# Row numbers of an edge step: spread over the partitions by TensorE, or read from DRAM as a broadcast

## The chip, the cores and the metric

One Trainium2 chip, one core of it. The metric is the device time of one execution in microseconds. The engines are TensorE (PE, with its weight loads shown as PEld), VectorE (DVE), ScalarE (ACT), GpSimd (POOL) and SyncE (SP), which here only issues DMA transfers and waits.

## The reference

The kernel computes one layer of a graph network on 6250 nodes of 256 channels with 200000 edges. Three parts are added to a residual:

```
xn = _layernorm(x, axis=-1)
x = x + _L0_gnn_ref(xn, src, dst, ...) + _L0_mix_ref(xn[None], ...)[0]
x = x + _L0_ffn_ref(_layernorm(x, axis=-1)[None], ...)[0]
```

The graph part is attention over edges: for each edge a score from its two end nodes, an exponential, and a sum of the weighted rows of one end node into the other ("row") node:

```
e = jnp.einsum('ehd,hd->eh', Wh_i, a_src) + jnp.einsum('ehd,hd->eh', Wh_j, a_dst)
e = jax.nn.leaky_relu(e, negative_slope=ALPHA)
e = jnp.exp(e - jnp.max(e, axis=0, keepdims=True))
e_sum = jax.ops.segment_sum(e, edge_row, num_segments=N)
alpha = e / (e_sum[edge_row] + 1e-15)
h_new = jax.ops.segment_sum(Wh_j * alpha[..., None], edge_row, num_segments=N)
```

The mix part is a linear attention over all nodes with products of pairs of channels as features. The last part is a layer of 8 experts of which each node uses two.

## The kernel before

**Stages.** First the nodes are projected in 49 tiles of 128 and stored in DRAM while the edges are sorted (to about 600 us). Then comes the stage that the change touches, from about 628 us to 3670 us. The experts follow.

**The edge stage.** The sorted edges are cut into 391 groups of 512 (GE = 512, four times 128 edges). A step is a pair of a group and a tile of 128 row nodes; there are 440 steps, written as 110 laps of four (a lap's step s has slot s). Each of the five engines runs its own program over the laps, and they meet at semaphores. For step k:

- POOL gathers the 512 node rows of the group from `table` with four indirect DMAs (L805), once for each group.
- DVE makes a one-hot matrix with edges on the partitions (one_hot, L1438).
- The row numbers of the group's 512 edges, counted from the tile's first row, are wanted on every partition. `rows_b` holds them for all steps: step 4p + b lies on partition p, block b. PE spreads one partition's 512 numbers over all partitions by a product with a column of the identity (spread_rows, L1911), into `pbank[0]`.
- ACT takes them in copy_oht: `away` = |number - partition| (L1028), then 1 - away, cut at zero (L1031). That is OHT, the one-hot matrix with row nodes on the partitions. Just before, it copies the tile's table (`rowt`, L1026).
- PE multiplies OHT with the tile's table (row_scores, L1924), DVE adds the gathered scores (scores, L1455 to L1458), ACT takes exponentials (exps, L1037), DVE weighs the gathered rows (weigh, L1464), PE sums them into rows (sum_rows, L1935), and DVE adds the sums into `agg` (add, L1475).

**Order.** Within step k the engines' queues are, in this order. PE: spread_rows(k+3), sum_rows(k), row_scores(k+2), then the step's share of the mix part. ACT: copy_oht(k+3), exps(k+1), then its share. DVE: weigh(k), its share, scores(k+1), add(k-1), one_hot(k+3). Spread_rows(k) waits until ACT has read the bank for step k-1 (`rows_taken`); copy_oht waits for the product (`rows_made`). All numbers go through one bank.

**The mix part** rides on the same laps. In the first 52 laps (K laps, four times 13) SP loads tiles of `kv_dram` (load_k), DVE makes features of them (L1484 to L1487) and PE sums products (kv_part, L1944). In the next 49 laps (Q laps) SP loads from `q_dram` (load_q), DVE makes features, PE transposes them (ft_part, L1969), ACT copies the transposes (L1076), PE multiplies them (y_part, L1977 and L1980). Spread over a lap are the tail of the tile before (copies L1057, L1052 and L1065 on ACT, L1512 and L1515 on DVE) and its store (store_mix). In Q laps ft_part stands between spread_rows and sum_rows. The last nine laps, 36 steps, have edges only.

**SP's queue.** It waits in order: load_k of unit j, s may go once PE has used the unit four before it, load_q once DVE has. Parameters of the last stage are loaded between the K passes (`early`, L576).

Of the kernel before, what the change touches and what calls it, by code (L numbers as in the profile page):

```python
# [139 lines left out]
def _build(nc, t, ctx):  # L140
# [3 lines left out]
    def sem(name):  # L144
        return ctx.enter_context(nc.semaphore(name))
# [11 lines left out]
    xs_dram = [nc.dram_tensor(f"xs_dram{b}", [n, C], F32).ap() for b, n in enumerate(XROWS)]  # L157
    y_dram = [nc.dram_tensor(f"y_dram{b}", [n * P, C], F32).ap() for b, n in enumerate(BTILES)]
    sorted_dram = nc.dram_tensor("sorted_dram", [P * KEYS // GE, GE], I32).ap()

# [12 lines left out]
    rows_b = spare[:, 2 * U * P:4 * U * P].bitcast(BF16).rearrange("p (a n) -> p a n", a=4)  # L173
    ident_b = sb("ident_b", [P, P], BF16)
    away = sb("away", [P, 2, GE], BF16)
# [199 lines left out]
    oh_done = sem("oh_done")  # L375
    rows_made = sem("rows_made")
    rows_taken = sem("rows_taken")
# [128 lines left out]
    def _(sp):  # L506
# [26 lines left out]


        for i in range(2):
            sp.wait_ge(st_out[i], 48 * ((NT + 1 - i) // 2))
# [30 lines left out]

        for pair in range(PAIRS):
            for s in range(4):
                load_k(pair, 0, s)  # L570
            with sp.Fori(1, KL - 1) as j:
                for s in range(4):
                    load_k(pair, j, s)
            load_k(pair, KL - 1, 0)
            for dst, src, loaded in early[pair::PAIRS]:
                sp.dma_start(dst, src, allow_slow_non_contiguous=True).then_inc(loaded, 16)  # L576
        for s in range(4):
            load_q(0, s)
        for s in range(4):
            load_q(1, s)  # L580
        with sp.Fori(2, NT) as q:
            for s in range(4):
                load_q(q, s)
            store_mix(q - 2)
        store_mix(NT - 2)
        store_mix(NT - 1)


# [314 lines left out]
    def _(act):  # L903
# [117 lines left out]
        def copy_oht(k):  # L1021
            s = k.slot
            if k.after(4):
                act.wait_ge(s_made, k.n - 3)
            i = act.value_load(istep[0:1, bass.ds(k.n, 1)], min_val=0, max_val=AGT - 1)
            o.mark(act.activation(rowt[:, s, :], row_pl[:, bass.ds(i, 1), :, :].rearrange("p a b n -> p (a b n)"), ACT.Copy))  # L1026
            act.wait_ge(rows_made, k.n + 1)
            o.mark(act.activation(away[:, s % 2, :], pbank[0][:, :], ACT.Abs, bias=minus_p[:, 0:1]))  # L1028
            o.settle()
            act.sem_inc(rows_taken, 1)  # L1030
            act.activation(OHT[:, s, :, :].rearrange("p u n -> p (u n)"), away[:, s % 2, :], ACT.Relu, scale=-1.0, bias=ones[:, 0:1]).then_inc(oht_done, 1)  # L1031
# [185 lines left out]
    def _(dve):  # L1217
# [186 lines left out]
        dve.sem_inc(s_pint, 1)  # L1404
        o.mark(dve.tensor_copy(rows_b[:, :, :], planf[:, 1, :, :]))
        o.mark(dve.tensor_copy(ident_b[:, :], ident[:, :]))

# [419 lines left out]
    def _(pe):  # L1827
# [77 lines left out]

        def spread_rows(k):

            if k.after(1):
                pe.wait_ge(rows_taken, k.n)
            one = ident_b[:, bass.ds(k.lap, 1)].to_broadcast([P, P])  # L1910
            pe.matmul(pbank[0][:, :], one, rows_b[:, k.slot, :], start=True, stop=True).then_inc(rows_made, 1)  # L1911

        def row_scores(k):
# [90 lines left out]
        def lap(i, extra=None, middle=None):  # L2004
            for s in range(4):
                k = At(i, s, 4)
                if (k + 3).inside(STEPS):
                    spread_rows(k + 3)
                if middle is not None:
# [13 lines left out]

        for s in range(3):
            spread_rows(At(0, s, 4))
        row_scores(At(0, 0, 4))
# [169 lines left out]
```

## Time and profile before

| | |
|---|---|
| time, three runs | 4551.9, 4566.98 and 4567.17 us (median 4566.98) |
| the profiled execution | 4563.81 us |
| its span in the trace | 4561.9 us |
| mean granted clock of TensorE | 0.844 of full |
| busy: PE, DVE, ACT, POOL | 73%, 59%, 39%, 56% of the span |
| edge stage | about 628 to 3670 us |
| HBM traffic | 308.82 MB read, 84.30 MB written |

The profile is of one execution. A busy share is a mean over stages with different limits; a wait is listed with the engine and line that released it, as far as the trace can tell. "Remote" and "another core or an unknown queue" stand for a releaser that it can't name, "issue" for time in which the engine waited for nothing that the profile shows. The clock is a share of 2.4 GHz: a stretch at 0.5 is at the lower level, 1.2 GHz, and a mean between is a mixture of the two. Some matmul records can be missing from a trace.

### The profile page before, as it was taken

What the parts mean: (1) busy time and instruction counts of PE and PEld (TensorE: products, weight loads), DVE (VectorE), ACT (ScalarE), POOL (GpSimd) and SP (SyncE); (2) the same over time, 40 slices, a digit from 0 to 9 for tenths busy, and PEclk for the clock granted to TensorE, in tenths of its full rate; (3) what the DMA queues carried; (4) which work ended last, traced back from release to release, by engine and by line L of the source; (5) the groups of instructions that cost most, each with busy time, mean ns of one, the idle gap of its engine ahead of it and who ended that gap; (6) DMA issues with size and microseconds to landing.
All of it is one profiled execution on the core that took longest, in us unless ns stands there. A gap on an engine that the chain in (4) does not pass through costs nothing.

```text
span 4561.9 us, 90761 instructions
## 1 busy us (share of the span) xinstructions
PE 3309.0 (73%) x23188; PEld 2345.3 (51%) x23505; DVE 2688.7 (59%) x6015; ACT 1791.1 (39%) x4855; POOL 2546.9 (56%) x2454
## 2 busy tenths in 40 slices
PE   5888747767767777777777777777776545877895
PEld 2333324444444444456665666666564435665785
DVE  9888876657667666655555555555554463534222
ACT  3666422223323223244444444444443212543563
POOL 4566457767778867755565555555555613234223
PEclk8676668879989979889888989989897776988998
DMA  2222123333333323322222222222222232334344
GB/s 66 77 76 77 60 84 90 87 94 91 98 93 94 106 78 91 98 73 73 70 76 68 73 75 72 71 75 71 68 74 64 72 127 71 110 105 146 97 133 138
DMA packets 260611, 394.74 MB, mean 87 GB/s; under 512 B 71952, under 2 KB 195022, under 8 KB 260232
## 3 DMA queue, kind: packets, MB, share of 16 engines
q0 software_dynamic: 86704, 239.52, 18.9%
q1 hardware_dynamic: 150924, 132.95, 9.4%
q10 hardware_dynamic: 22860, 20.83, 1.6%
q8 instruction: 53, 0.87, 0.1%
q14 instruction: 70, 0.57, 0.0%
HBM read 308.82 MB, written 84.30 MB: 86 GB/s over the span
## 4 chain that ended last, share of the span: by engine, by line
PE 29%; issue 20%; DVE 13%; another core or an unknown queue 12%; DVEq 12%; ACT 7%; POOL 4%; ACTq 2%; DMA 1%; POOLq 0%; SPq 0%
PE bank L1935 6%; PE bank L1856 5%; DVEq L1445 4%; DVEq L1468 4%; PE bank L2123 3%; PE bank L2135 3%; DVEq L1444 3%; PE bank L1858 2%; PE bank L1969 2%; ACT away L1028 2%; DVE room L1438 1%; POOL room L805 1%; PE bank L1924 1%; DVE room L1464 1%
## 5 line engine op out<-in xcount | busy, mean ns | idle before, releaser
L805 POOL DMA_INDIRECT room<-table,room x1564 | 1804.0, 1153 | 1091.6 <-DVE room L1464 645.5
L1935 PE MATMUL bank<-room 128*128 128x260 f32 x3520 | 1020.7, 439 | 380.3 <-issue 208.0
L1935 PEld LDWEIGHTS bank<-room 128*128 128x128 f32 x3520 | 730.5, 218 | 512.0 <-issue 398.9
L1484 DVE TENSOR_TENSOR room<-room 128x1024 f32<-128x1024 f32 x392 | 481.2, 1228 | 533.0 <-issue 499.1
L1464 DVE TENSOR_TENSOR room<-room 128x1024 f32<-128x1024 f32 x440 | 537.0, 1220 | 389.7 <-ACT room L1037 268.4
L1028 ACT ACTIVATE away<-bank,minus_p 128x512 bf16<-128x512 f32 x440 | 301.7, 686 | 1084.7 <-remote 980.2
L1969 PE MATMUL bank<-ident,room 128*128 128x128 f32 x1764 | 262.1, 299 | 206.6 <-DVE room L1487 142.7
L1856 PE MATMUL bank<-room 128*128 128x264 f32 (+1 forms) x588 | 312.8, 673 | 65.8 <-issue 34.4
L1031 ACT ACTIVATE spare<-away,ones 128x512 bf16<-128x512 bf16 x440 | 317.6, 722 | 54.2
L1969 PEld LDWEIGHTS bank<-ident,room 128*128 128x128 f32 x1764 | 218.6, 154 | 197.1 <-issue 185.6
L1924 PE MATMUL bank<-rowt,spare 128*128 128x8 bf16 x7040 | 262.1, 167 | 73.2 <-issue 72.5
L1438 DVE TENSOR_TENSOR room<-iota_f,row_step 128x512 f32<-128x512 f32 x440 | 308.0, 700 | 0.3 <-DVE row_step L1376 0.3
L2135 PE MATMUL bank<-room 128*128 x952 | 243.4, 400 | 57.8 <-issue 22.4
L1944 PE MATMUL bank<-room 128*33 128x64 f32 (+1 forms) x1568 | 267.1, 447 | 13.2 <-DVE room L1487 6.5
L1769 DVE TENSOR_TENSOR planes<-bank,spare 128x256 f32<-128x256 f32 x119 | 50.5, 425 | 374.9 <-PE bank L2135 237.5
L1924 PEld LDWEIGHTS bank<-rowt,spare 128*128 128x128 bf16 x7040 | 214.6, 97 | 93.2 <-issue 80.8
L1076 ACT ACTIVATE room<-bank 128x512 f32<-128x512 f32 (+1 forms) x588 | 247.8, 486 | 21.1 <-remote 10.0
L1037 ACT ACTIVATE room<-room 128x16 f32<-128x16 f32 x440 | 92.2, 209 | 416.7 <-issue 188.0
L1980 PE MATMUL bank<-room,kvm 128*33 128x128 f32 x3136 | 247.1, 302 | 6.1 <-issue 5.8
L2123 PE MATMUL bank<-room 128*128 128x128 f32 x1904 | 242.0, 280 | 12.9 <-issue 12.9
L1856 PEld LDWEIGHTS bank<-room 128*128 128x128 f32 x588 | 138.8, 260 | 200.4 <-issue 144.1
L2123 PEld LDWEIGHTS bank<-room 128*128 128x128 f32 x1904 | 231.0, 197 | 12.9 <-issue 12.9
(313 smaller groups left out, 4793.0 us busy)
## 6 DMA issues: line engine op xcount, KB each, us to landing
room<-table,room POOLq DMA_INDIRECT x1564
kv_dram<-room SPq DMA_DIRECT2D x49, 324.0 KB, 2.2
room<-kv_dram SPq DMA_DIRECT2D x196, 81.0 KB
y_dram<-planes SPq DMA_DIRECT2D x119, 128.0 KB
room<-xs_dram ACTq DMA_DIRECT2D x110, 128.0 KB
q_dram<-room SPq DMA_DIRECT2D x49, 192.0 KB, 1.8
room<-q_dram SPq DMA_DIRECT2D x196, 48.0 KB
table<-room SPq DMA_DIRECT2D x49, 130.0 KB, 2.1
```

The source lines that it names most:

```text
L805: pool.indirect_dma_start(G[:, k.slot, u, :], None, table, bass.IndirectOffsetOnAxis(ap=ixbuf[:, k.slot, u:u + 1].bitcast(I32), axis=0)).t ...
L1028: o.mark(act.activation(away[:, s % 2, :], pbank[0][:, :], ACT.Abs, bias=minus_p[:, 0:1]))
L1031: act.activation(OHT[:, s, :, :].rearrange("p u n -> p (u n)"), away[:, s % 2, :], ACT.Relu, scale=-1.0, bias=ones[:, 0:1]).then_inc(oht_d ...
L1438: dve.tensor_tensor(OH[:, s, :, :], iota_f[:].unsqueeze(1).to_broadcast([P, U, P]), row_step[:, bass.ds(k.n, 1), :].rearrange("p a u -> p ...
L1464: dve.tensor_tensor(Gw[:, h, :, 0:C].rearrange("p u (h d) -> p u h d", h=GH), G[:, bass.ds(slot, 1), :, 0:C].rearrange("p a u (h d) -> p ( ...
L1484: dve.tensor_tensor(f.rearrange("p h (d i) -> p h d i", i=MD), over(x, [[XD, 2], [0, h], [1, MD]]), over(x, [[XD, 2], [1, h], [1, MD]]), A ...
L1856: ins = pe.matmul(out, xnT[:, s, c, :], w[:, c, :], start=(c == 0), stop=(c == 1 and bias is None))
L1924: ins = pe.matmul(out[:, u * w:(u + 1) * w], OHT[:, s, u, :], rowt[:, s, j * w:(j + 1) * w], start=False, stop=(j == 3), skip_group_check= ...
L1935: ins = pe.matmul(pbank[1 + h][:, 0:TW], OH[:, s, u, :], Gw[:, h, u, :], start=(u == 0), stop=(u == U - 1))
L1969: ins = pe.transpose(pbank[3 + j][:, x * P:(x + 1) * P], src, ident[:])
L2123: ins = pe.matmul(pbank[4 + n % 2][:, c * P:(c + 1) * P], w1_t[:, n % 2, kc * HID + c * P:kc * HID + (c + 1) * P], xT_t[:, n % 2, kc, :], ...
L2135: ins = pe.matmul(pbank[6 + n % 2][:, 0:C], h_t[:, n % 2, c, :], w2[:, bass.ds(e, 1), c, :].rearrange("p a n -> p (a n)"), start=(c == 0), ...
```

## The change

The row numbers no longer pass through PE. Once DVE has cast them into `rows_b`, SP writes that tile to DRAM (`rows_dram`, one line of 512 numbers for each step). For each step SP then issues one DMA that reads the step's line and writes it to all 128 partitions, into one of four slots of `rows_b`, which is used over again for this. ACT's `away` reads the slot in SBUF in place of the PSUM bank and waits for the load's semaphore (`row_in`). Load k waits until ACT has taken step k-4. The loads are placed between SP's other transfers, about one lap ahead of the step. Spread_rows, the identity in bfloat16 and the semaphore `rows_made` go.

```diff
--- before.py
+++ after.py
@@ -156,6 +156,7 @@
     x1_dram = nc.dram_tensor("x1_dram", [NP, C], F32).ap()
     xs_dram = [nc.dram_tensor(f"xs_dram{b}", [n, C], F32).ap() for b, n in enumerate(XROWS)]
     y_dram = [nc.dram_tensor(f"y_dram{b}", [n * P, C], F32).ap() for b, n in enumerate(BTILES)]
+    rows_dram = nc.dram_tensor("rows_dram", [PLAN, GE], BF16).ap()
     sorted_dram = nc.dram_tensor("sorted_dram", [P * KEYS // GE, GE], I32).ap()
 
 
@@ -171,7 +172,6 @@
     spare = sb("spare", [P, XE * C])
     OHT = spare[:, 0:2 * U * P].bitcast(BF16).rearrange("p (a u n) -> p a u n", a=4, u=U)
     rows_b = spare[:, 2 * U * P:4 * U * P].bitcast(BF16).rearrange("p (a n) -> p a n", a=4)
-    ident_b = sb("ident_b", [P, P], BF16)
     away = sb("away", [P, 2, GE], BF16)
     minus_p = sb("minus_p", [P, 1])
     rowt = sb("rowt", [P, 4, 4 * 2 * GH], BF16)
@@ -373,7 +373,8 @@
     gathered = [sem(f"gathered{i}") for i in range(4)]
     landed = sem("landed")
     oh_done = sem("oh_done")
-    rows_made = sem("rows_made")
+    s_rows = sem("s_rows")
+    row_in = [sem(f"row_in{i}") for i in range(4)]
     rows_taken = sem("rows_taken")
     oht_done = sem("oht_done")
     s_made = sem("s_made")
@@ -532,6 +533,17 @@
         sp.dma_start(sorted_dram.rearrange("(p g) e -> p (g e)", p=P), key[SORTED][:, :].bitcast(I32)).then_inc(s_sorted_out, 16)
 
 
+        def load_row(k):
+
+            if k.after(4):
+                sp.wait_ge(rows_taken, k.n - 3)
+            sp.dma_start(rows_b[:, k.slot, :], rows_dram[bass.ds(k.n, 1), :].rearrange("a n -> (a n)").partition_broadcast(P)).then_inc(row_in[k.slot], 16)
+
+        sp.wait_ge(s_rows, 1)
+        sp.dma_start(rows_dram.rearrange("(p b) e -> p b e", b=4), rows_b[:, :, :]).then_inc(s_rows, 16)
+        sp.wait_ge(s_rows, 17)
+        for s in range(4):
+            load_row(At(0, s, 4))
         for i in range(2):
             sp.wait_ge(st_out[i], 48 * ((NT + 1 - i) // 2))
         sp.wait_ge(s_plan, 1)
@@ -566,24 +578,33 @@
         early += [(w2[:, e, :, :], t["W2"][e].rearrange("(c p) n -> p c n", p=P), s_w4e) for e in range(XE)]
 
         for pair in range(PAIRS):
+            l0 = pair * KL
             for s in range(4):
                 load_k(pair, 0, s)
+                load_row(At(l0 + 1, s, 4))
             with sp.Fori(1, KL - 1) as j:
                 for s in range(4):
+                    load_row(At(j + (l0 + 1), s, 4))
                     load_k(pair, j, s)
             load_k(pair, KL - 1, 0)
+            for s in range(4):
+                load_row(At(l0 + KL, s, 4))
             for dst, src, loaded in early[pair::PAIRS]:
                 sp.dma_start(dst, src, allow_slow_non_contiguous=True).then_inc(loaded, 16)
-        for s in range(4):
-            load_q(0, s)
-        for s in range(4):
-            load_q(1, s)
+        for q in range(2):
+            for s in range(4):
+                load_q(q, s)
+                load_row(At(LAPS_K + q + 1, s, 4))
         with sp.Fori(2, NT) as q:
             for s in range(4):
+                load_row(At(q + (LAPS_K + 1), s, 4))
                 load_q(q, s)
             store_mix(q - 2)
         store_mix(NT - 2)
         store_mix(NT - 1)
+        with sp.Fori(LAPS_K + NT + 1, LAPS) as i:
+            for s in range(4):
+                load_row(At(i, s, 4))
 
 
         sp.wait_ge(s_edges_end, 1)
@@ -1024,8 +1045,8 @@
                 act.wait_ge(s_made, k.n - 3)
             i = act.value_load(istep[0:1, bass.ds(k.n, 1)], min_val=0, max_val=AGT - 1)
             o.mark(act.activation(rowt[:, s, :], row_pl[:, bass.ds(i, 1), :, :].rearrange("p a b n -> p (a b n)"), ACT.Copy))
-            act.wait_ge(rows_made, k.n + 1)
-            o.mark(act.activation(away[:, s % 2, :], pbank[0][:, :], ACT.Abs, bias=minus_p[:, 0:1]))
+            act.wait_ge(row_in[s], 16 * (k.lap + 1))
+            o.mark(act.activation(away[:, s % 2, :], rows_b[:, s, :], ACT.Abs, bias=minus_p[:, 0:1]))
             o.settle()
             act.sem_inc(rows_taken, 1)
             act.activation(OHT[:, s, :, :].rearrange("p u n -> p (u n)"), away[:, s % 2, :], ACT.Relu, scale=-1.0, bias=ones[:, 0:1]).then_inc(oht_done, 1)
@@ -1402,8 +1423,7 @@
             o.mark(dve.tensor_scalar(planf[:, 1, b, :], plan[:, b, :].bitcast(I32), pc[:, 8 + b:9 + b], None, ALU.subtract))
         o.settle()
         dve.sem_inc(s_pint, 1)
-        o.mark(dve.tensor_copy(rows_b[:, :, :], planf[:, 1, :, :]))
-        o.mark(dve.tensor_copy(ident_b[:, :], ident[:, :]))
+        dve.tensor_copy(rows_b[:, :, :], planf[:, 1, :, :]).then_inc(s_rows, 1)
 
         dve.wait_ge(qkn_done, NT)
         for i in range(2):
@@ -1903,13 +1923,6 @@
                 z = zero_b[:].unsqueeze(1).to_broadcast([P, 4, P]) if w == MAIN else zero_b[:, 0:w]
                 pe.matmul(pbank[bnk][:, 0:w], zero_b[:], z, start=True, stop=False, skip_group_check=True)
 
-        def spread_rows(k):
-
-            if k.after(1):
-                pe.wait_ge(rows_taken, k.n)
-            one = ident_b[:, bass.ds(k.lap, 1)].to_broadcast([P, P])
-            pe.matmul(pbank[0][:, :], one, rows_b[:, k.slot, :], start=True, stop=True).then_inc(rows_made, 1)
-
         def row_scores(k):
 
             s, h = k.slot, k.slot % 2
@@ -2004,8 +2017,6 @@
         def lap(i, extra=None, middle=None):
             for s in range(4):
                 k = At(i, s, 4)
-                if (k + 3).inside(STEPS):
-                    spread_rows(k + 3)
                 if middle is not None:
                     middle(s)
                 sum_rows(k)
@@ -2021,8 +2032,6 @@
                 y_part(q, s)
             return extra
 
-        for s in range(3):
-            spread_rows(At(0, s, 4))
         row_scores(At(0, 0, 4))
         row_scores(At(0, 1, 4))
         for pair in range(PAIRS):
```

## Rows read from the trace of the kernel before

**Rows 1.** The page, part 4: the chain of waits by engine
```profile
PE 29%; issue 20%; DVE 13%; another core or an unknown queue 12%; DVEq 12%; ACT 7%; POOL 4%; ACTq 2%; DMA 1%; POOLq 0%; SPq 0%
```

**Rows 2.** Busy time by stretch: us, PE, PEld, DVE, ACT, POOL, clock, DMA share, GB/s
```profile
640.00:1926.00 1286.00, 924.86 (x6850) 575.89 (x6953) 848.98 (x2055) 375.51 (x837) 960.55 (x919) 0.87 0.35 93
1940.00:3442.00 1502.00, 1151.97 (x10598) 919.97 (x10792) 849.69 (x2046) 657.57 (x1549) 839.21 (x870) 0.90 0.26 72
3457.00:3672.00 215.00, 126.91 (x872) 90.43 (x888) 96.24 (x242) 59.39 (x134) 124.75 (x138) 0.74 0.26 70
```

**Rows 3.** Waits, DVE, 640 to 1926 us: total, times, longest
```profile
DVE room L1464 <- ACT room L1037: 29.6, 18, 3.6
```

**Rows 4.** Waits, DVE, 1940 to 3442 us
```profile
DVE room L1464 <- ACT room L1037: 234.4, 78, 5.6
```

**Rows 5.** Waits, ACT, 1940 to 3442 us
```profile
ACT away L1028 <- remote: 497.1, 169, 7.9
ACT room L1052 <- remote: 65.7, 16, 5.0
ACT room L1052 <- PE bank L1996: 57.2, 27, 3.8
ACT room L1065 <- remote: 47.5, 9, 9.4
```

**Rows 6.** Line L1911: count, duration ns min/median/max
```profile
L1911 PEld LDWEIGHTS bank<-spare,ident_b x440: 95/96/152, 627.4 to 3660.3; 128*128 x133, 128*128 128x128 bf16 x14
...
L1911 PE MATMUL bank<-spare,ident_b x123: 376/390/615, 629.2 to 3657.5; 128*128 128x512 bf16 x123
```

**Rows 7.** Timeline of one Q step: start, duration, engine, [idle before <-releaser]
```profile
2486.43 0.10 PEld L1911 LDWEIGHTS bank<-spare,ident_b 128*128 x1 [0.20 <-issue]
...
2487.64 1.92 PE L1935 MATMUL bank<-room 128*128 128x260 f32 x8
...
2488.25 0.16 DVE L1458 TENSOR_TENSOR room<-room,bank 128x16 f32<-128x16 f32 x1
...
2491.33 0.69 ACT L1028 ACTIVATE away<-bank,minus_p 128x512 bf16<-128x512 f32 x1 [2.86 <-remote]
...
2492.77 0.20 ACT L1037 ACTIVATE room<-room 128x16 f32<-128x16 f32 x1
...
2493.11 1.22 DVE L1464 TENSOR_TENSOR room<-room 128x1024 f32<-128x1024 f32 x1 [3.70 <-ACT room L1037]
```

**Rows 8.** Waits, PE, 1940 to 3442 us
```profile
PE bank L1969 <- DVE room L1487: 142.0, 113, 5.5
PE bank L1977 <- ACT room L1076: 93.6, 59, 2.6
```

**Rows 9.** Line L1935 by stretch: us, PE, PEld, clock, DMA share, GB/s
```profile
640.00:1926.00 1286.00, 496.32 (x1656) 349.41 (x1656) 0.87 0.35 93
1940.00:3442.00 1502.00, 417.78 (x1560) 307.50 (x1560) 0.90 0.26 72
3457.00:3672.00 215.00, 97.91 (x277) 67.66 (x278) 0.74 0.26 70
```

**Rows 10.** Waits, DVE, 3457 to 3672 us
```profile
DVE room L1455 <- PE bank L1924: 30.2, 6, 12.5
```

**Rows 11.** The page, part 5: busy, mean ns of one, idle before
```profile
L1028 ACT ACTIVATE away<-bank,minus_p 128x512 bf16<-128x512 f32 x440 | 301.7, 686 | 1084.7 <-remote 980.2
...
L1031 ACT ACTIVATE spare<-away,ones 128x512 bf16<-128x512 bf16 x440 | 317.6, 722 | 54.2
```

**Rows 12.** DMA issues over the run: KB each, median us to landing
```profile
spare<-in_b SPq DMA_DIRECT2D x1, 1024.0 KB, 12.2
```

**Rows 13.** DMA queues, 640 to 1926 us: packets, MB, share of 16 engines
```profile
q0 software_dynamic: 35265, 97.86, 28.0%
q1 hardware_dynamic: 34384, 20.87, 6.4%
```

**Rows 14.** Waits, POOL, 640 to 1926 us
```profile
POOL room L805 <- DVE room L1464: 119.3, 24, 12.5
```

## The prediction

> **What bounds the kernel now.** I read the chain of waits over the whole run first [rows 1]: TensorE (PE) 29%, but 12% is "another core or an unknown queue", on one core. That is a wait whose releaser the trace doesn't name. The reader is to see that no engine's throughput sets the end.
>
> Then the busy time in three windows of the stage that the change touches [rows 2]: the K laps (208 steps, 1286 us, 6.2 us a step), the Q laps (196 steps, 1502 us, 7.7 us a step) and the last 36 steps (215 us). PE is busy 72%, 77% and 59% of them, VectorE (DVE) 66%, 57% and 45%. GpSimd (POOL) is busy 75% in the K laps and 56% in the Q laps. In the K laps DVE and POOL are each nearly full once their register loads and issue gaps are added; in the Q laps something else is late.
>
> Then the waits, by stage. DVE's weigh (L1464) waits for ScalarE's (ACT's) exponentials (L1037) 29.6 us in the K laps [rows 3] and 234.4 us in the Q laps, 78 times [rows 4]. Why are the exponentials late? ACT runs copy_oht(k+3) ahead of exps(k+1), and copy_oht waits for the product that spreads the row numbers: away (L1028) waits 497.1 us in the Q laps on a "remote" releaser [rows 5]. It is the product: L1911 ran 440 times and only 123 of its matmuls are recorded, so mostly the trace can't name it [rows 6]. The timeline of one Q step shows the damage [rows 7]: the weights of the product are loaded at 2486.43, the input of the exponentials (L1458) is ready at 2488.41, but away starts only at 2491.33, the exponentials at 2492.77, and weigh 3.70 us late. The product itself is 0.4 us; the hand-over from PE to ACT took 4.9 us. ACT's other waits for PE, L1052 and L1065, are late in the same manner [rows 5], so I put it down to PE's side and not to ACT's.
>
> **The change, part by part.**
>
> *The product goes* (440 times 0.39 us, the median of the recorded ones [rows 6]), and with it ACT's dependence on PE's place in its queue.
> Q laps: 234.4 us [rows 4] is the most that earlier exponentials give at weigh. ACT waits ahead of them for away (497.1) and for the tail copies (65.7 + 57.2 + 47.5 = 170.4) [rows 5]; away's share is 497/667 = 0.75, so 175 us. Not all of it survives. PE has 1502 - 1152 = 350 us of recorded idle, in which lie the unrecorded products (196 times 0.39 = 76 us); it waits 142.0 us of it for features (L1969 on L1487) and 93.6 for ACT's copies (L1977 on L1076) [rows 2, 8]. A step that is 175/196 = 0.9 us shorter uses most of what PE has free, with its issue gaps, so PE ends last in part of the steps. I take 0.7 of 175: -125 us, bounds 0 and -234.
> K laps: weigh waits 29.6 us for exponentials; I take 20. Where PE's clock is low PE can end last: sum_rows (L1935) is 300 ns here, against 240 and about 479 at the two levels (8 of them took 1.92 us in the step of [rows 7]; half the clock doubles it), so a quarter of the steps, 52, are slow, times 0.4 us is 21 us, of which I take half [rows 7, 9]. Together -30 us, bounds 0 and -50.
> Last 36 steps: L1455 waits 30.2 us for row_scores (L1924) [rows 10]. Row_scores waits for OHT, which comes after away. I take -10 us, bounds 0 and -30: that wait may also be PE's own.
>
> *PE's wait for rows_taken goes, too.* It was met early nearly always; nothing.
>
> *away now reads SBUF.* L1028 from PSUM takes 686 ns, L1031 of the same size from SBUF 722 [rows 11]: +0.036 us times 440 = 16 us on ACT, which is 29% to 44% busy in the windows [rows 2]. I take +5 us, bounds 0 and +16.
>
> *SP's loads.* 440 loads of 128 copies of 1 KB. Load k+4 is issued once away of step k is done and is needed by away of step k+4, four steps or 25 to 31 us later. The one broadcast in the trace, 1024 KB, landed in 12.2 us [rows 12]; an eighth of it is far inside the lead even if the fixed part were all of it. Behind a waiting load_row in SP's queue stand load_k or load_q and store_mix. In the loops load_k of step k was free once PE had used unit k-4; now it also waits for away of step k, which ACT does three steps before DVE wants the unit, so 18 us are left: hidden. Store_mix(NT-1) now has the last rows behind it, once; ACT needs the next row about a step later, so 0 to 5 us. At the start the row numbers go to DRAM (512 KB, half of 12.2 us by [rows 12]) and the first row comes back before the first away, while DVE makes the other tables: 0 to +8 us, I take +2. DVE's ident_b copy, under 0.3 us, goes.
>
> *The 16 DMA engines.* The SP queue's packets took 6.4% of 16 x 1286 us for 34384 packets of 607 bytes, 38 ns each; POOL's took 28.0% for 35265 of 2775 bytes, 163 ns [rows 13]. By the line between them 1 KB is 63 ns, so a row load is 128 x 63 / 16 = 0.5 us on every DMA engine, about 8 points of share on top of 35% in the K laps. The other bound is 12.2/8 = 1.5 us. The gathers share these engines. In the K laps POOL waits 119.3 us for weigh, its slack; its 919 instructions are 184 groups of one index copy and four gathers, so 0.65 us a group [rows 2, 14]. A load delays a group by 0.5 x 208/184 = 0.57 us at most by the first bound: under the slack, +5 us. I take the first because its packets are nearest in kind.
>
> Sum: -125 - 30 - 10 + 5 + 2 + 5 = -153 us. The profiled execution took 4563.8 us (span 4561.9), 3 us under the median 4567.0. **4411 us**, 3.4% faster.
>
> **The rivals.**
>
> *A. The next engine takes over.* In the Q laps DVE's features and PE's own work come next. For it: PE waits 142 us for features already [rows 8], and POOL and DVE are near full in the K laps. Against it: the K laps, with the same weigh, features and scores on DVE, take 6.2 us a step [rows 2]. Gain then about 50 us: 4515.
>
> *B. It doesn't do what it says: away stays late.* If the late start is ACT's (its sequencer) and the product only stands beside it, the wait moves to the load's semaphore. For it: 4.9 us isn't a matmul's time. Against it: L1052 and L1065, which PE releases too, wait for "remote" as well [rows 5], and in [rows 7] ACT goes from away (2491.33) to the exponentials (2492.77) in 1.44 us, which is the two passes of 0.7 us [rows 11] without a gap. 4564 plus ACT's 5: 4569.
>
> *C. The row loads hold up the gathers: slower.* Place: the K laps, where POOL is nearly full. At 1.5 us on every DMA engine a group lands 1.7 us later: 184 x (1.7 - 0.65) = +193 us, against -153 with its DMA term taken out (-158): 4599, and the more the worse. It decides from a delay of 0.65 + 158/184 = 1.5 us a group. For it: 128 reads of the same 1 KB, which the trace never shows at this rate. Against: the 16 DMA engines are 26% to 35% busy [rows 2].
> The Trainium skill, "DMA: Bandwidth & Descriptors", section "Issuing engines are not separate DMA queues", says that another issuing engine brings no DMA engines of its own; by it SP's loads and POOL's gathers compete, which is this rival, and leaves its price open.
>
> *D. PE's clock falls.* The granted clock is 0.87, 0.90 and 0.74 in the three windows, and L1935 takes 300, 268 and 353 ns [rows 2, 9]. Where PE does least (59%) it is lowest. Without the products PE is idle 5% more of a step unless the step shrinks as well. If the Q laps came halfway to the last window, PE's 1152 us grow by 0.16, 184 us, half behind DVE: +92, and the gain from an early away is half lost with it: 4564 - 90 + 92 = 4566, and as slow as 4600 with the K laps.
> The Trainium skill, "TensorE: Matmul & The Clock Gate", section "What's actually happening", says that "the default state is throttled, and activity releases the throttle". By it work taken from PE can cost clock; the sum without the rule is 4411, with it 4566.
>
> **How the numbers follow.** Chances: forecast 0.60 (its own range 4320 to 4490), A 0.15, B 0.10, C 0.11, D 0.04. No change is within 0.5%, 23 us, about what a measurement of this kernel tells. Faster: the forecast, A but for a little: 0.74. Same: B, half of D, some of A: 0.13. Slower: C and the rest of D: 0.13. The range: 4290, where weigh's 234 us and 50 of the K laps are all saved, to 4575, which takes in B; left out are C, half of D and a tail of the forecast, about 2 in 10.
>
> **What would show it.** Right: in the Q laps L1464's wait for L1037 falls from 234 to under 80 us and the steps to about 7.0 us; away (L1028) waits next to nothing for its release anywhere; the K laps shrink by under 3%; the DMA share rises by 6 to 9 points, POOL's wait for weigh shrinks. B: away still waits hundreds of us. C: L1455 waits for landed in the K laps, POOL waits for its own gathers. D: granted clock under 0.85 in the Q laps. Wrong altogether: away waits for row loads that come late, or SP hands out load_q too late, seen in L1484's waits.

## The result and the profile after

| kernel | median us | executions | ratio to before |
|---|---|---|---|
| before | 4559.4 | 4 | |
| changed | 4378.7 | 4 (4348.7 to 4399.9) | 0.960 [0.953, 0.967] |

4.0% faster, 181 us, against 153 predicted. The profiled execution of the changed kernel is the quickest of its four (4348.7), so distances between the two profiles come out some 30 us longer than those between the medians. Its lines moved: away is L1049 (was L1028), the relu behind it L1052 (L1031), exponentials L1058 (L1037), scores L1475 to L1478 (L1455 to L1458), weigh L1484 (L1464), sum_rows L1948 (L1935), row_scores L1937 (L1924), PE's transposes for features L1982 (L1969), ACT's copies of them L1097 (L1076), gathers L826 (L805), load_row L540.

The page of the changed kernel: the chain of waits, away and the relu (busy, mean ns, idle before), and the row loads.

```profile
PE 27%; issue 24%; DVE 16%; DVEq 16%; ACT 5%; POOL 5%; another core or an unknown queue 4%; ACTq 1%; DMA 1%; POOLq 0%; SPq 0%
...
L1052 ACT ACTIVATE spare<-away,ones 128x512 bf16<-128x512 bf16 x440 | 317.6, 722 | 54.0
...
L1049 ACT ACTIVATE away<-spare,minus_p 128x512 bf16<-128x512 bf16 x440 | 312.7, 711 | 0.1
...
spare<-rows_dram SPq DMA_DIRECT2D x440, 128.0 KB
```

The nameless releaser went from 12% of the chain [rows 1] to 4%. Away's idle time went from 1084.7 us [rows 11] to 0.1.

The same three stretches of the changed kernel, K laps, Q laps and last steps, columns as in [rows 2]:

```profile
634.00:1873.00 1239.00, 899.33 (x6764) 563.65 (x6764) 848.91 (x2055) 370.30 (x838) 973.20 (x918) 0.87 0.46 118
1890.00:3222.00 1332.00, 1094.15 (x10572) 864.20 (x10573) 845.21 (x2047) 661.99 (x1551) 882.72 (x868) 0.96 0.39 100
3237.00:3454.00 217.00, 128.20 (x859) 92.13 (x858) 97.09 (x244) 59.50 (x135) 123.27 (x138) 0.73 0.36 89
```

Before and after, each stage from the start of its first weigh to the start of its last: first weigh at 639.7 and 634.2; K laps 1286.3 and 1238.5 (-47.8); Q laps 1502.6 and 1331.8 (-170.8); last 36 steps 215.6 and 216.0; all behind them 889.4 and 893.8. The two steps between these stretches took 28.4 us together and 32.6. A Q step fell from 7.7 to 6.8 us. The granted clock in the Q laps rose from 0.90 to 0.96.

What DVE, ACT and PE of the changed kernel wait for in the Q laps (us in total, times, longest):

```profile
DVE room L1484 <- ACT room L1058: 78.7, 51, 4.2
...
DVE room L1475 <- remote: 36.1, 19, 5.6
```

```profile
ACT room L1097 <- remote: 147.0, 67, 4.3
...
ACT room L1073 <- remote: 52.2, 19, 5.0
ACT room L1073 <- PE bank L2009: 41.1, 21, 3.7
```

Weigh's wait for exponentials is a third of its 234.4 [rows 4]. What is left of it has the same look: ACT's copies of PE's results (L1097 for features, L1073 in the tail) still wait for "remote" for up to 5 us, and exponentials queue behind them.

The DMA queues in the K laps, and what POOL and SP wait for there:

```profile
q0 software_dynamic: 35231, 97.75, 29.6%
q1 hardware_dynamic: 64249, 48.10, 16.3%
```

```profile
POOL room L826 <- DVE room L1484: 46.9, 9, 11.3
POOL room L826 <- DMA room<-table,room: 32.3, 48, 3.3
```

SP's queue has 64249 - 34384 = 29865 packets more than [rows 13], 144 a load where I had counted 128, and its share of the 16 engines rose from 6.4% to 16.3%: (0.163 x 16 x 1239 - 0.064 x 16 x 1286) / 29865 = 64 ns a packet, against 63 predicted. POOL's wait for weigh fell from 119.3 us [rows 14] to 46.9, and in its place stands a wait for its own gathers, 32.3 us.

So far the forecast seems to stand. But "the hand-over from PE to ACT" was only a name for 4.9 us in a timeline. What in it is slow: PE's work, PE's place in its queue, or the signal, that is, the step of the semaphore by which PE tells ACT that a product is ready?

### The profile page after: what moved, and what is told of

Same layout as the page of the kernel before. It is cut to its first block, busy times and chain, and to the rows that moved or that the text cites. A ratio compares the mean times of both kernels' runs of the same rounds, so it can differ in the third digit from the quotient of the medians.

```text
span 4346.9 us, 91344 instructions
## 1 busy us (share of the span) xinstructions
PE 3221.4 (74%) x23065; PEld 2275.9 (52%) x23065; DVE 2682.9 (62%) x6014; ACT 1788.8 (41%) x4855; POOL 2601.5 (60%) x2454
## 4 chain that ended last, share of the span: by engine, by line
PE 27%; issue 24%; DVE 16%; DVEq 16%; ACT 5%; POOL 5%; another core or an unknown queue 4%; ACTq 1%; DMA 1%; POOLq 0%; SPq 0%
PE bank L1948 6%; DVEq L1465 6%; PE bank L1876 5%; DVEq L1488 4%; DVEq L1464 4%; PE bank L2132 3%; PE bank L2144 3%; PE bank L1878 2%; DVE room L1504 2%; POOL room L826 2%; DVE room L1458 2%; PE bank L1982 1%; DVE room L1484 1%; POOL xs_dram L885 1%
## 5 line engine op out<-in xcount | busy, mean ns | idle before, releaser
L826 POOL DMA_INDIRECT room<-table,room x1564 | 1849.6, 1183 | 814.2 <-issue 413.7
L1948 PE MATMUL bank<-room 128*128 128x260 f32 x3520 | 1021.4, 439 | 389.6 <-issue 221.3
L1948 PEld LDWEIGHTS bank<-room 128*128 128x128 f32 x3520 | 728.7, 218 | 540.2 <-issue 425.8
L1484 DVE TENSOR_TENSOR room<-room 128x1024 f32<-128x1024 f32 x440 | 536.9, 1220 | 208.7 <-issue 130.0
L1058 ACT ACTIVATE room<-room 128x16 f32<-128x16 f32 x440 | 94.1, 214 | 1131.7 <-issue 456.4
L1982 PE MATMUL bank<-ident,room 128*128 128x128 f32 x1764 | 256.8, 295 | 154.9 <-DVE room L1507 122.9
L1052 ACT ACTIVATE spare<-away,ones 128x512 bf16<-128x512 bf16 x440 | 317.6, 722 | 54.0
L1097 ACT ACTIVATE room<-bank 128x512 f32<-128x512 f32 (+1 forms) x588 | 250.6, 490 | 177.7 <-remote 147.0
L1982 PEld LDWEIGHTS bank<-ident,room 128*128 128x128 f32 x1764 | 206.8, 150 | 206.6 <-issue 206.6
L1049 ACT ACTIVATE away<-spare,minus_p 128x512 bf16<-128x512 bf16 x440 | 312.7, 711 | 0.1
L1458 DVE TENSOR_TENSOR room<-iota_f,row_step 128x512 f32<-128x512 f32 x440 | 306.3, 697 | 0.3 <-issue 0.3
L1937 PE MATMUL bank<-rowt,spare 128*128 128x8 bf16 x7040 | 259.8, 167 | 41.1 <-issue 40.6
L1937 PEld LDWEIGHTS bank<-rowt,spare 128*128 128x128 bf16 x7040 | 213.7, 97 | 58.8 <-issue 45.7
L1993 PE MATMUL bank<-room,kvm 128*33 128x128 f32 x3136 | 229.1, 285 | 10.7 <-issue 10.6
```

What stands on the lines that cost most here:

```text
L826: pool.indirect_dma_start(G[:, k.slot, u, :], None, table, bass.IndirectOffsetOnAxis(ap=ixbuf[:, k.slot, u:u + 1].bitcast(I32), axis=0)).t ...
L1049: o.mark(act.activation(away[:, s % 2, :], rows_b[:, s, :], ACT.Abs, bias=minus_p[:, 0:1]))
L1458: dve.tensor_tensor(OH[:, s, :, :], iota_f[:].unsqueeze(1).to_broadcast([P, U, P]), row_step[:, bass.ds(k.n, 1), :].rearrange("p a u -> p ...
L1484: dve.tensor_tensor(Gw[:, h, :, 0:C].rearrange("p u (h d) -> p u h d", h=GH), G[:, bass.ds(slot, 1), :, 0:C].rearrange("p a u (h d) -> p ( ...
L1937: ins = pe.matmul(out[:, u * w:(u + 1) * w], OHT[:, s, u, :], rowt[:, s, j * w:(j + 1) * w], start=False, stop=(j == 3), skip_group_check= ...
L1948: ins = pe.matmul(pbank[1 + h][:, 0:TW], OH[:, s, u, :], Gw[:, h, u, :], start=(u == 0), stop=(u == U - 1))
```

## The experiments

Kernels were measured on several chips, each beside the kernel before on the same chip, and the chips turned out to differ. A ratio here is always to the kernel before on its own chip.

**1. Which part of the hand-over costs (chip on which before takes 4474.6 us).** Three kernels put one piece of the removed product back into the changed kernel. The first computes a full product of zeros in PE's old place, and no one waits for it:

```diff
+        def spread_rows(k):
+            pe.matmul(pbank[0][:, :], zero_b[:], zero_b[:].unsqueeze(1).to_broadcast([P, 4, P]), start=True, stop=True)
...
+                if (k + 3).inside(STEPS):
+                    spread_rows(k + 3)
```

The second computes 8 columns there, and away waits for that product as well as for its row load:

```diff
+            act.wait_ge(rows_made, k.n + 1)
...
+            pe.matmul(pbank[0][:, 0:8], zero_b[:], zero_b[:, 0:8], start=True, stop=True).then_inc(rows_made, 1)
```

The third has the same wait, but PE computes nothing; its sequencer raises the semaphore when it comes to that place in its queue:

```diff
+            pe.sem_inc(rows_made, 1)
```

The fourth is the changed kernel again, as control.

> The changed kernel plus PE's 440 products of 512 columns in the old place of its queue, of zeros, into the same bank, which nobody reads or waits for. Theory T (the gain is ACT's wait for PE's signal): about 4395 us, at most 40 over the changed kernel's 4379, and away still starts without a wait. Rival W (the gain is PE's own 0.4 us a step): 4500 to 4560 us.

> The changed kernel plus a product of 8 columns in the old place of PE's queue, and away waits for its signal beside the row load's. T: back to 4500 to 4560 us, away waits hundreds of us in the Q laps, though PE does nearly no work for it. W: 4380 to 4400 us.

> As the one before, but PE only raises the semaphore from its queue at that place, with no matmul. If the lateness is that of a finished matmul's signal (T1), away is released when PE's queue gets there and the time is 4380 to 4440 us; if it is PE's place in its queue, which comes late (T2), the time is that of the small product, 4500 to 4560 us.

> The changed kernel itself, on the same chip as the three above, so that they can be compared: 4350 to 4400 us under every theory.

| kernel | median us | ratio to before | against the control |
|---|---|---|---|
| changed (control) | 4316.1 | 0.966 [0.961, 0.970] | |
| product that no one reads | 4318.9 | 0.966 [0.961, 0.970] | +3 |
| 8-column product, waited for | 4545.7 | 1.017 [1.012, 1.021] | +230 |
| place in the queue, waited for | 4347.7 | 0.971 [0.966, 0.975] | +32 |

The control came out at 4316 us, below the 4350 to 4400 that I expected: this chip is quicker than the first one, so only the distances to the control count. PE's 440 products cost nothing. Waiting for PE's sequencer to come to that place costs 32 us. Waiting for the end of a product of 8 columns at that place costs 230, more than the change had gained on this chip (158). What hurts is the wait for a finished matmul, and not its work.

The idle time before away over the whole run, by what ended it; first with the 8-column product, then with the bare semaphore:

```profile
  remote: 591.9, 137
  PE bank L1930: 343.8, 193
```

```profile
  PEq L1930: 116.9, 110
```

A timeline of the kernel with the 8-column product, Q laps (start, duration; in brackets the idle time before it):

```profile
2254.22 0.18 PE L1930 MATMUL bank<-zero_b 128*128 128x8 bf16 x1
...
2254.72 1.20 PE L1988 MATMUL bank<-ident,room 128*128 128x128 f32 x9 [0.31 <-issue]
...
2255.75 1.92 PE L1954 MATMUL bank<-room 128*128 128x260 f32 x8
...
2258.71 0.42 PE L1943 MATMUL bank<-rowt,spare 128*128 128x8 bf16 x11 [0.52 <-issue]
...
2258.83 0.72 ACT L1051 ACTIVATE away<-spare,minus_p 128x512 bf16<-128x512 bf16 x1 [7.23 <-remote]
...
2260.64 1.22 DVE L1486 TENSOR_TENSOR room<-room 128x1024 f32<-128x1024 f32 x1 [3.42 <-ACT room L1060]
```

By the trace the product is over at 2254.40 and away starts at 2258.83, 4.4 us later, while PE has run 17 transposes and sums and begun the next scores. Its row load had come long before, and ACT stood idle for 7.23 us. Weigh pays 3.42. This is the picture of [rows 7], with a product a 64th as wide. Elsewhere in the same run away starts 0.23 us after the product began (2295.38 and 2295.61). The Trainium skill, "Perfetto Trace Analysis", section "Tensor Engine Instruction (MATMUL, LD_WEIGHTS)", says that a matmul's reported end is computed, and that its semaphore follows only when PSUM has acknowledged all writes; the 4.4 us lie behind the end so computed, and no run here shows on which side of the acknowledgement.

The 32 and the 230 us don't split the cost into place and signal, because the bare semaphore is raised at an earlier time than a product in its place could run. One step of that kernel:

```profile
2303.74 1.07 PE L1999 MATMUL bank<-room,kvm 128*33 128x128 f32 x16
2304.01 0.72 ACT L1051 ACTIVATE away<-spare,minus_p 128x512 bf16<-128x512 bf16 x1 [0.93 <-PEq L1930]
```

L1999 stands ahead of the semaphore in PE's queue, and away starts while PE is still at it. So it is in all 92 waits of the Q laps that the sequencer ended. In the kernel with the 8-column product ACT stood idle before away for 958 us, 346 times: 439 us of it before the product's computed end, 519 us behind it; in 124 of the 346 away started less than 0.3 us after that end, in 167 more than 1 us. The wait is thus for PE to come to the product about as much as for a late signal, and what each alone would cost was not measured.

**2. The urgent work first instead.** If a late signal ahead of the exponentials is what costs, moving exps(k+1) ahead of copy_oht(k+3) in ACT's queue should give the kernel before most of the gain, and the changed one, where exponentials still queue behind the tail copies, 1 to 2%.

```diff
             for s in range(4):
...
+                if (k + 1).inside(STEPS):
+                    exps(k + 1)
                 if (k + 3).inside(STEPS):
                     copy_oht(k + 3)
-                if (k + 1).inside(STEPS):
-                    exps(k + 1)
```

> The kernel before with one swap in ACT's queue: exps(k+1) stands ahead of copy_oht(k+3), so a late away no longer holds up the exponentials. If the late exponentials are how the late signal costs time (T), this gives most of the change's gain without any DMA: 4340 to 4420 us where the kernel before takes 4475 on the last chip, and weigh waits under 60 us for exponentials in the Q laps. If the gain has another way (PE waiting for OHT), it stays within 1% of before.

> The changed kernel with the same swap. Exponentials still start 1.4 and 1.8 us after their input in two of the four slots of a Q lap, because ACT does the tail copies and copy_oht first. T: 1 to 2% faster than the changed kernel (ratio to before about 0.95). Rival (PE ends last in the Q laps now, the swap only delays OHT): within 0.5% of the changed kernel, ratio 0.966.

| before takes | kernel | median us | ratio |
|---|---|---|---|
| 4079.5 | before, exponentials first | 4051.8 | 0.993 [0.991, 0.994] |
| 4079.5 | changed, exponentials first | 4081.0 | 1.000 [0.999, 1.001] |

These ran on another chip, on which the kernel before takes 4079 us, 480 less than in the first comparison, and where the order alone was worth 0.7%: that is the rival's range (within 1%), not the one that I expected. The changed kernel in that order was no faster than before, which neither theory had. Either order, or chip. So I ran the changed kernel as it is, and both reordered ones, on a third chip, and the reordered kernel before once more on a chip where before takes 4567 us.

> The changed kernel again, since the chips differ: 4560 and 4475 us for the kernel before on two of them and 4079 on a third, where ACT saw PE's signals at once. T with late signals as the cause: where the kernel before takes about 4080, this takes 4080 to 4110 (ratio 1.00 to 1.01: no signal to wait for, only the loads' cost is left); where it takes 4450 or more, the ratio is 0.96 to 0.97. Rival (the gain is the same share on every chip): 0.96 to 0.97 on any.

> The kernel before with exponentials ahead of copy_oht, again. On a chip with prompt signals 0.9925 as measured; on one with late signals T says 0.95 to 0.97 (it takes the late away off the exponentials' path), the rival (OHT is what PE waits for) 0.99 or more.

> The changed kernel with the same swap, again. On a chip with prompt signals 1.00 as measured; on one with late signals 0.94 to 0.96, since the tail copies and copy_oht no longer stand before the exponentials.

> The kernel before with exponentials ahead of copy_oht, a last time, for a chip with late signals. There T says 0.95 to 0.97, the rival (PE waits for OHT instead) 0.99 or more. On a chip with prompt signals it tells nothing new: 0.991 to 0.993.

| before takes | kernel | median us | ratio |
|---|---|---|---|
| 4087.6 | changed | 4116.0 | 1.006 [1.004, 1.008] |
| 4087.6 | before, exponentials first | 4048.8 | 0.991 [0.989, 0.992] |
| 4087.6 | changed, exponentials first | 4088.4 | 1.000 [0.999, 1.001] |
| 4567.4 | before, exponentials first | 4476.3 | 0.980 [0.973, 0.987] |

The sign of the change depends on the chip: 4.0% and 3.4% faster where before takes 4559 and 4475 us, 0.6% slower where it takes 4088. The reordered kernel before, at 0.980 on the chip of 4567 us, falls between the two ranges (0.95 to 0.97, or 0.99 and more) and confirms neither. The traces show what differs. In the Q laps' tail ACT copies two transposes of PE as soon as it may (L1052 of the kernel before). The idle time before that copy on the 4088 us chip, in the reordered kernel before, and one of those copies:

```profile
  PE bank L1996: 26.3, 49
```

```profile
2007.16 0.42 PE L1996 MATMUL bank<-ident,room 128*128 128x128 f32 x2
...
2007.61 0.38 ACT L1052 ACTIVATE room<-bank 128x256 f32<-128x256 f32 x1 [0.45 <-PE bank L1996]
```

The transposes end at 2007.58 and the copy starts at 2007.61. Over such copies on the two chips of 4079 and 4088 us, where ACT stood ready, it starts 0.03 to 0.04 us after their end on average, at most 0.1. Where before takes 4475 us or more, the mean of each trace is 0.7 to 2.5 us and its longest 1.5 to 6.2, and the same wait of the kernel before has a nameless releaser 16 times [rows 5]. So "remote" in these rows is PE's signal, seen late. I call the two kinds prompt-signal and late-signal chips from here on. Not every signal is late on the latter (15 of the 46 such copies of the kernel before start within 0.1 us), and in the first stage ACT's copies of PE's transposes (L938) start 0.04 us after them on both kinds.

Away shows it in one and the same kernel, before with exponentials first, on the chips of 4088 and 4567 us:

```profile
L1028 ACT ACTIVATE away<-bank,minus_p 128x512 bf16<-128x512 f32 x440 | 295.1, 671 | 1.0 <-remote 0.8
```

```profile
L1028 ACT ACTIVATE away<-bank,minus_p 128x512 bf16<-128x512 f32 x440 | 297.1, 675 | 243.7 <-remote 235.5
```

Where signals are prompt, ACT almost never waits for the product, from the same place in PE's queue. So neither the signal nor PE's place in its queue costs ACT anything there. Whether PE comes late to the product on the other chips because of late signals elsewhere was not tested.

Where signals are prompt, the reordered pair shows what the change costs by itself. K and Q laps of before with exponentials first, then of the changed kernel with exponentials first, both where before takes 4088 us:

```profile
632.00:1829.00 1197.00, 885.50 (x6851) 563.18 (x6954) 846.54 (x2055) 361.97 (x836) 989.30 (x917) 0.90 0.37 99
1840.00:3026.00 1186.00, 1033.46 (x10572) 854.65 (x10767) 837.82 (x2047) 653.50 (x1551) 928.51 (x873) 0.99 0.34 92
```

```profile
639.00:1851.00 1212.00, 878.07 (x6764) 557.98 (x6764) 847.37 (x2055) 370.03 (x838) 991.34 (x918) 0.87 0.46 121
1864.00:3057.00 1193.00, 1050.61 (x10569) 847.18 (x10570) 838.23 (x2047) 659.82 (x1551) 925.02 (x874) 0.97 0.43 112
```

4048.8 to 4088.4 is +40 us (in the old order it is +28, 4087.6 to 4116.0): +7 until the first weigh, +14 in the K laps, +3 between them and the Q laps, +7 in the Q laps, +9 in the last steps. The DMA share is 9 points higher in both stages, and the clock a little lower. The swap itself is worth 28 us to the changed kernel on this chip, 39 us to the one before.

On the late-signal chip the reordered kernel before gained 91 us, 2.0%, about half of the change's 4%. Its ACT and PE in the Q laps:

```profile
ACT away L1028 <- remote: 220.9, 112, 5.7
```

```profile
PE bank L1977 <- ACT room L1076: 148.0, 128, 3.3
```

Away still waits, and now the feature copies behind it are what is late: PE waits 148.0 us for them, against 93.6 [rows 8]. Reordering moves the wait off weigh's path; the change removes it.

**3. The row loads twice (before 4079.5 us).** From the second lap on, each row load is issued a second time into a tile that no one reads:

```diff
             sp.dma_start(rows_b[:, k.slot, :], rows_dram[...]...).then_inc(row_in[k.slot], 16)
+            if k.after(4):
+                if not (k.fixed() and k.lap == 1):
+                    sp.wait_ge(unread_in[k.slot], 16 * (k.lap - 1))
+                sp.dma_start(unread[:, k.slot, :], rows_dram[...]...).then_inc(unread_in[k.slot], 16)
```

> The changed kernel with every row load from the second lap on issued a second time, into a tile that nobody reads. If the loads are covered (my sum's 5 us), at most +15 us over the changed kernel, ratio to before 0.966 to 0.970. If they already hold up gathers (rival C in small), the second set costs 40 us or more, ratio 0.975 and up, and POOL's gathers or landed show waits in the K laps.

4205.6 us, 1.031 [1.029, 1.032]. I expected 15 us at most; the rival had 40 us or more. If the changed kernel, which was not run on this chip, stands at 1.006 of before as on the other prompt-signal chip, the second load costs about 100 us. Its profile is 83 us longer than that of the changed kernel on the other prompt-signal chip; 63 of them lie in the K laps and 23 in the last steps, and the Q laps are no longer. K and Q laps with two loads a step:

```profile
639.00:1911.00 1272.00, 895.73 (x6758) 569.81 (x6758) 848.30 (x2052) 372.86 (x844) 972.32 (x920) 0.85 0.55 137
1925.00:3154.00 1229.00, 1042.35 (x10562) 848.72 (x10562) 837.38 (x2039) 654.19 (x1548) 904.43 (x875) 0.97 0.55 130
```

POOL's idle time before a gather that an earlier gather's landing ended, over the run: with no row loads (before, exponentials first), with one a step (changed, exponentials first), and with two:

```profile
  DMA room<-table,room: 36.5, 93
```

```profile
  DMA room<-table,room: 66.0, 113
```

```profile
  DMA room<-table,room: 269.9, 194
```

30 us more for the first load (13 in the changed kernel in its own order, with 49.3), 204 for the second, at DMA shares of 0.37, 0.46 and 0.55 in the K laps. That is rival C's mechanism: the row loads hold up the gathers, long before the 16 engines are full, and the second load does so much more than the first.

**4. The product later in PE's queue, in the kernel before (before 4079.5 us).** To take the run of short matmuls away from ahead of the product, it was moved behind sum_rows(k):

```diff
-                if (k + 3).inside(STEPS):
-                    spread_rows(k + 3)
                 if middle is not None:
                     middle(s)
                 sum_rows(k)
+                if (k + 3).inside(STEPS):
+                    spread_rows(k + 3)
```

> The kernel before with spread_rows(k+3) moved behind sum_rows(k) in PE's queue: there 8 long matmuls stand directly ahead of it, not the 17 short ones of row_scores and 17 or 34 of the mix part. If the signal is late because a run of short matmuls stands ahead of it in PE (S1), away starts within 0.8 us of the product in over 80% of the steps that wait. If any matmul's signal is late (S2), the share stays under 60%. The time can go either way, since the product now also waits for weigh: 4400 to 4540 us on this scale.

5452.7 us, 1.336 [1.333, 1.338], far outside what I expected, and by another mechanism. DVE's wait over the whole run, and one step:

```profile
DVE room L1464 <- ACT room L1037: 1309.8, 323, 7.7
```

```profile
2603.34 2.85 PE L1935 MATMUL bank<-room 128*128 128x260 f32 x8
...
2605.81 0.10 PEld L1911 LDWEIGHTS bank<-spare,ident_b 128*128 x1
...
2606.44 0.69 ACT L1028 ACTIVATE away<-bank,minus_p 128x512 bf16<-128x512 f32 x1 [7.99 <-remote]
...
2607.88 0.20 ACT L1037 ACTIVATE room<-room 128x16 f32<-128x16 f32 x1
...
2608.22 1.23 DVE L1464 TENSOR_TENSOR room<-room 128x1024 f32<-128x1024 f32 x1 [5.34 <-ACT room L1037]
```

The signal is prompt: the product's weights at 2605.81, away at 2606.44. The releaser is called "remote" here as well, because most products have no record [rows 6]: for this line the name alone doesn't tell a late signal. But sum_rows(k) waits for weigh(k), the product for sum_rows(k), away for the product, exps(k+1) for away and weigh(k+1) for exps(k+1): every step is one serial chain through three engines. In the Q laps the step's features and their transposes, which stand ahead of sum_rows, are in that chain too, and there it costs most: against the reordered kernel before on the same chip the K laps took 1384.2 us for 1196.6, the Q laps 2325.3 for 1185.2. PE is recorded busy for 68% of the Q laps there, against 87%, and the granted clock is 0.71, against 0.99.

It says nothing on whether short matmuls make a signal late, since it ran on a chip where none is. It does show that a low clock alone doesn't make one late: in all 437 steps in which ACT waited, away started within 1.0 us of the end of the product's weight load.

## Why the prediction was right, and where it was not

- **The mechanism.** "The hand-over from PE to ACT", put down to PE's side: right. It is the wait for a finished product (+230 us with 8 columns) and not PE's own work (+3). How much of it is a late signal and how much PE's place in its queue stays open: of ACT's idle time 519 us lay behind the product's computed end and 439 us before it. What the prediction could not see is that the wait belongs to some chips only. The 4.0% holds for those; where signals are prompt there is little to remove, and the change's costs remain. That the forecast was made and measured where the wait exists is luck.
- **Q laps, -125.** Mis-sized: -171. The 175 us that I first worked out from away's share of ACT's waits nearly all came, and the factor 0.7 for PE ending last was wrong. Weigh's wait fell by 156. PE did not become the bound: with its 440 products put back (experiment 1) the time was the same. Its clock rose from 0.90 to 0.96, and its recorded busy time fell by 58 us.
- **K laps, -30 + 5.** Mis-sized: -48. I had counted weigh's 29.6 us [rows 3] and PE's own time. PE's time was worth nothing (experiment 1). What I had left out is one step further down: scores (L1455) waited 45.3 us for a nameless releaser in the K laps, of which 19.6 are left, probably because row_scores needs OHT, which comes from away (rows below, before and after).

```profile
DVE room L1455 <- remote: 45.3, 10, 7.4
```

```profile
DVE room L1475 <- remote: 19.6, 10, 6.0
```

- **Last 36 steps, -10.** Measured 0, which the bound allowed. An early away didn't shorten the wait for row_scores: it is 54.1 us by name there now, against 30.2 [rows 10], and 26.4 by a nameless releaser, against 39.9.
- **Away from SBUF.** 711 ns against 686 [rows 11]: +11 us on ACT in all, inside the bounds, hidden.
- **The loads.** Always in time: away waits 0.1 us. The price of a packet was right (64 ns). SP waits 1084.7 us for ACT's releases of the row tiles (row behind this item), and no engine waits for what stands behind in its queue. The DMA share rose by 11 and 13 points, not 6 to 9: a load is 144 packets, not 128, the laps are shorter, and the gathers' own packets take 29.6% where they took 28.0% [rows 13]. The sum's costs (5 + 2 + 5 = 12 us) were too low by a factor of two to three, 28 to 40 us where signals are prompt (7 of the 40 at the start, for which I had taken 2): in the main C's mechanism, far below its deciding point.

SP's longest wait in the changed kernel, over the run:

```profile
SPq L540 <- ACTq L1051: 1084.7, 250, 11.6
```

- **Rival A** (next engine takes over, 50 us gained): refuted on late-signal chips. **B** (away stays late): refuted, 0.1 us. **D** (clock falls): refuted in the Q laps, where it rose; on a prompt-signal chip it did fall, 0.99 to 0.97, inside the 40 us. **C** (slower): wrong in sign on late-signal chips; right in sign on the prompt-signal one, with 28 to 40 us instead of its 193.
- **Two errors of opposite sign.** The medians differ by 181 us. If the costs are 40 us here too, which was measured on another chip, the gain before costs was 221, where I had 165: 56 too small, against costs 28 too small, so the total was off by 28 only. So near a hit is in part luck.

Which version is best depends on the chip, too: with prompt signals the kernel before with exponentials first (0.991 and 0.993), with late ones the changed kernel (0.960 and 0.966), against 0.980 for the reordered kernel before, though the three come from different comparisons and the changed kernel was not run beside the reordered one on such a chip. The changed kernel with exponentials first was not run on a chip with late signals. Open is also what makes a chip's signals late.

## What to carry to other kernels

Where one engine waits in the middle of its queue for a matmul's result, the price is the wait and not the matmul: a product of 8 columns was no cheaper to wait for than one of 512. Put what the path needs ahead of that wait, or take the value from somewhere else than PE. A small broadcast load in every step is not free beside gathers that are nearly late, though the DMA engines are half idle; double it once to see how steep the price is. And measure a change that is about hand-overs on more than one chip before calling it a gain.

## What the runs showed of the hardware

- The same kernel took 4079, 4088, 4475, 4559 and 4567 us on different chips or in different comparisons. Of the 480 us between the ends, some 50 lie in the last stage (889 us on a late-signal chip, 835 to 838 on prompt-signal ones), where PE's results are handed on as well, and most in the stage treated here.
- On late-signal chips ACT saw the end of PE's transposes in the Q laps 0.7 to 2.5 us late on average and up to 6.2, on the prompt-signal ones 0.03 to 0.04 and at most 0.1; in the first stage it was 0.04 on both. A semaphore raised by PE's sequencer cost +32 us on a late-signal chip, where the matmul's cost +230; it was raised while matmuls ahead of it in the queue still ran.
- A low granted clock did not make signals late on a prompt-signal chip: 0.71 in the Q laps of experiment 4, and away within 1.0 us of the end of the product's weight load.
- In the Q laps with the 8-column product, the 68 waits that ended over 1 us after the product had 35 to 42 matmuls started in the 3 us ahead of it. Of the 107 that ended within 0.5 us, 65 had 18 to 27 and 42 had 32 to 41. So many short matmuls ahead don't suffice for a late signal. That is one trace; the K laps show no such difference, and no experiment tested it.
- A row load of 128 packets of 1 KB, and 16 more, took 64 ns of a DMA engine per packet. One a step cost at most 40 us over the kernel (all else that the change costs is in it), a second one about 100 more.
